# Four transposed pieces or one: turning back the weighted values in layers three and four of an eight-block transformer kernel

## The reference, cut to what matters

```python
# 16 heads of 8 channels, for each head and query
p = exp(q @ k.T * scale - row_max)          # masked: a window of 64, or causal
o = (p @ v) / p.sum(-1)                     # weighted values over the sum of weights
x = x + o.reshape(T, 128) @ W_o             # projection and residual
```

## Time and profile before

| | us |
|---|---|
| runs | 1268.28, 1269.37, 1276.36 |
| median | 1269.37 |
| profiled execution, first to last instruction (span) | 1288.7 |
| of it, layers three and four up to the routing's end, about | 520 to 1190 |

### The profile page before, as it was taken

The page is one execution under the profiler, slowest core; times in us unless marked ns, Lnnn a source line. Parts: engine busy times, 40 slices in busy tenths (PEclk is TensorE's granted clock), DMA queues, the critical chain, the costliest instruction groups (busy, mean ns, idle before and its releaser), DMA issues.

```text
span 1288.7 us, 39126 instructions
## 1 busy us (share of the span) xinstructions
PE 1079.1 (84%) x16755; PEld 784.4 (61%) x16755; DVE 832.1 (65%) x2425; ACT 551.8 (43%) x993; POOL 448.7 (35%) x538
## 2 busy tenths in 40 slices
PE   6989868999976996887888888888888888897994
PEld 4767647888864673644555656565555655453884
DVE  6888674678974213367768786877858685635332
ACT  3332102366552331324473836556374645361442
POOL 3134341436655253122221333142223203012575
PEclk9898869999986998898999999998999999898998
DMA  9554505652240413103021222211122201101884
GB/s 369 203 214 176 202 27 180 199 177 87 71 162 31 136 54 94 47 26 89 18 76 37 53 81 54 61 47 55 45 61 61 64 6 27 42 13 61 214 199 91
DMA packets 85167, 126.05 MB, mean 98 GB/s; under 512 B 14465, under 2 KB 66050, under 8 KB 84578
## 3 DMA queue, kind: packets, MB, share of 16 engines
q1 hardware_dynamic: 68258, 106.47, 25.8%
q0 software_dynamic: 10928, 13.64, 4.4%
q10 hardware_dynamic: 5808, 3.43, 1.1%
HBM read 50.82 MB, written 46.74 MB: 76 GB/s over the span
## 4 chain that ended last, share of the span: by engine, by line
PE 44%; DVE 22%; issue 9%; ACT 7%; DMA 6%; SPq 4%; POOL 4%; another core or an unknown queue 1%; ACTq 0%; DVEq 0%; POOLq 0%
DVE mx L1714 5%; SPq L2238 3%; PE ps L1058 3%; PE ps L1025 3%; ACT MW L1998 3%; PE ps L790 2%; PE ps L777 2%; PE ps L778 2%; PE ps L613 2%; PE ps L739 2%; DMA K<-spm 2%; ACT MW L1985 2%; DVE bst L1137 2%; PE ps L965 1%; DVE MW L1516 1%
## 5 line engine op out<-in xcount | busy, mean ns | idle before, releaser
L1714 DVE TENSOR_REDUCE mx<-ps 128x2 f32<-128x1024 f32 (+3 forms) x176 | 191.8, 1122 | 64.2 <-PE ps L1025 60.0
L1998 ACT ACTIVATE MW<-ps 128x1024 f32<-128x1024 f32 x160 | 154.6, 1036 | 87.8 <-PE ps L1042 87.3
L2136 POOL DMA_INDIRECT xs<-xr,sidu x96 | 97.1, 1011 | 134.2 <-DVE sidu L1296 99.1
L2079 POOL TENSOR_SCALAR rst<-bmv 128x4 f32<-128x4 f32 x64 | 16.3, 255 | 267.4 <-DVE bmv L1140 266.4
L1025 PE MATMUL ps<-K,Q 64*128 64x512 bf16 (+3 forms) x512 | 66.9, 324 | 27.7 <-DMA K<-spm 16.8
L1058 PE MATMUL ps<-MW,Vp 128*18 128x128 f32 x2560 | 88.5, 281 | 1.7 <-ACT MW L1998 1.2
L1058 PEld LDWEIGHTS ps<-MW,Vp 128*18 128x18 f32 x2560 | 65.0, 100 | 12.8 <-issue 4.7
L2162 POOL DMA_INDIRECT out_dram<-qf,toku x39 | 60.6, 1555 | 34.5 <-DVE toku L1770 25.9
L1985 ACT ACTIVATE MW<-ps 128x1024 f32<-128x1024 f32 x64 | 61.8, 1028 | 17.5 <-PE ps L951 15.3
L1042 PE MATMUL ps<-Q,K 64*128 64x128 bf16 x1280 | 55.9, 220 | 14.7 <-ACT MW L1998 7.1
L1803 ACT COPY XT<-ps 128x512 f32<-128x512 f32 x48 | 28.3, 590 | 87.9 <-PE ps L613 78.3
(11 more groups left out here) (381 smaller groups left out, 2606.5 us busy)
## 6 DMA issues: line engine op xcount, KB each, us to landing
xs<-hb SPq DMA_DIRECT2D x52, 528.0 KB, 8.6
MW<-l_moe_dram SPq DMA_DIRECT2D x19, 768.0 KB
MW<-l_moe_dram SPq DMA_DIRECT2D x20, 578.0 KB
Q<-spl SPq DMA_DIRECT2D x48, 128.0 KB
Q<-spm SPq DMA_DIRECT2D x48, 128.0 KB
K<-spl SPq DMA_DIRECT2D x43, 128.0 KB
K<-spm SPq DMA_DIRECT2D x43, 128.0 KB
MW<-l_moe_dram SPq DMA_DIRECT2D x16, 256.0 KB
```

The costliest lines, as they stand in the source:

```text
L1714: V.tensor_reduce(out=mx[1][:, :, s0:s0 + ns, t], in_=p.rearrange("p (e n) -> p e n", e=2)[:, :, 0:ns * nk].rearrange("p e (s k) -> p e s ...
L1998: A.activation(P3[k % 2][:, 1024 * half:1024 * half + 1024], p, ACT.Exp).then_inc(drained[u], 1)
L2136: G.indirect_dma_start(out=xs[L], out_offset=bass.IndirectOffsetOnAxis(ap=sidu[:, 4 * b + t:4 * b + t + 1], axis=0), in_=src[:, t, :], in_ ...
```

## The change

The four pieces become one step, `l2_t` or `l3_t`. It waits for the four tiles in turn, turns all eight halves into one unit (the full two banks), and DVE then takes one reciprocal of 64 numbers per partition and one product of 512. There are 16 such steps instead of 64. The step stands in the lists of PE and DVE where the last of its four pieces stood; with the pieces left out, all five engines' lists are the same step for step. `l3_t` of the last block keeps the two throw-away matmuls, now ahead of all eight transposes.

```diff
@@ ORDER2, one line of PE's list of many
-        l3_lat l3_q l3_e2 l3_b1 l3_k l3_e3 l3_b2 l3_v l3_t0 l2_m3 l3_e4 l3_b3 l3_t1 l3_e5 l3_b4 l2_n2 l3_e6 l3_b5 l3_e7 l2a_n l3_b6 l3_m0 l3_e8
...
-            ("l3_n2", B - 1): 4, ("l3_t3", B - 1): 2, ("l3f_n", B - 1): 3}
+            ("l3_n2", B - 1): 4, ("l3_t", B - 1): 2, ("l3f_n", B - 1): 3}
...
-    UNITS |= {f"{_t}_t{_i}": 1 for _i in range(4)} | {_t + "_u": 1, _t + "_j": 1}
+    UNITS |= {_t + "_t": 1, _t + "_u": 1, _t + "_j": 1}
@@ PE
-            def out_t(key, l, t):
+            def out_t(key, l):
                 u, n, p = unit(key)
-                rows = opb[l][t]
                 ahead(key)
-                e.wait_ge(og_out[l], 4 * key[1] + t + 1)
-                for g in range(2):
-                    m = PE.transpose(p[:, 128 * g:128 * g + 128], rows[:, g, :], ident)
+                for t in range(4):
+                    e.wait_ge(og_out[l], 4 * key[1] + t + 1)
+                    for g in range(2):
+                        m = PE.transpose(p[:, 256 * t + 128 * g:256 * t + 128 * g + 128], opb[l][t][:, g, :], ident)
                 m.then_inc(filled[u], 1)
@@ DVE
-            def out_t(key, l, t):
+            def out_t(key, l):
                 u, n, p = unit(key)
-                k = 4 * l + t
-                pv = p[:, 0:256].rearrange("p (q r) -> p q r", q=8)[:, :, 0:18].rearrange("p q (k e) -> p q k e", k=2)
-                rd = rdens[k].rearrange("p (q k) -> p q k", q=8)
-                if t == 0 and key[1]:
+                pv = p.rearrange("p (q r) -> p q r", q=32)[:, :, 0:18].rearrange("p q (k e) -> p q k e", k=2)
+                rd = rden[:, 64 * l:64 * l + 64].rearrange("p (q k) -> p q k", q=32)
+                if key[1]:
                     ukey = (key[0][:2] + "_u", key[1] - 1)
                     e.wait_ge(filled_of(ukey), after(ukey))
                 e.wait_ge(filled[u], n + 1)
                 own.end(V.reciprocal(rd, pv[:, :, :, 8]))
                 settled()
-                V.tensor_tensor(out=tcs[l][:, t, :].rearrange("p (q k e) -> p q k e", q=8, k=2), in0=pv[:, :, :, 0:8], in1=bc(rd, 3, [128, 8, 2, 8]),
+                V.tensor_tensor(out=tcs[l].rearrange("p t (q k e) -> p (t q) k e", q=8, k=2), in0=pv[:, :, :, 0:8], in1=bc(rd, 3, [128, 32, 2, 8]),
                                 op=ALU.mult).then_inc(drained[u], 1)
```

More of the change, by code:

```diff
@@ L219 @@
-        l3_m21 l3_n2 l3_e0 l3_e1 l3_b0 l3f_n l3_e2 l3_b1 l3t_r l3_e3 l3_t0 l3_b2 l3_e4 l3_b3 l3_e5 l3_b4 l3_e6 l3_b5 l3_t1 l3_e7 l3_b6 l3_e8 l3t_c
-        l3_b7 l3_e9 l3_b8 l3_t2 l3_b9 l3_t3 l3_u l3_j l3f_n l3t_r l3t_c
+        l2a_n l2_q l2a_n l2_v l2_m0 l2_m1 l2_m2 l2_m3 l2_n2 l2_q l2_e0 l2_e1 l2_o0 l2_e2 l2_o1 l2_e3 l2_o2 l2_o3 l2_t l2_u l2_j l2_v l2f_n l2f_0
+        l2f_1 l2f_2 l2_m0 l2f_o l2_m1 l2_m2 l3a_n l3_q l3_lat l2a_n l3_k l2_m3 l2_q l3_v l2_n2 l3_m0 l3_m1 l3_m2 l3_m3 l3_m4 l2_e0 l3_m5 l2_e1 l3_m6
@@ new lines @@
+        l3_m7 l2_o0 l3_m8 l2_e2 l3_m9 l3_m10 l2_o1 l3_m11 l3_m12 l2_o2 l3_m13 l2_e3 l3_m14 l3_m15 l2_o3 l2_t l3_m16 l2_u l3_m17 l2_j l3_m18 l2_v
+        l3_m19 l2f_n l3_m20 l3_m21 l2f_0 l2f_1 l2f_2 l3_n2 l2_m0 l2f_o l3_e0 l2_m1 l3_e1 l3_b0 l3a_n l2_m2 l3_lat l3_q l3_e2 l3_b1 l3_k l3_e3 l3_b2
+        l3_v l2_m3 l3_e4 l3_b3 l3_e5 l3_b4 l2_n2 l3_e6 l3_b5 l3_e7 l2a_n l3_b6 l3_m0 l3_e8 l3_b7 l3_m1 l3_e9 l3_b8 l3_m2 l3_m3 l2_q l3_m4 l3_b9 l3_m5
+        l2_e0 l3_m6 l2_e1 l3_m7 l3_m8 l2_o0 l3_m9 l2_e2 l3_m10 l2_o1 l3_m11 l2_e3 l3_m12 l3_m13 l2_o2 l3_t l3_m14 l2_o3 l3_m15 l3_u l2_t l3_m16
@@ new lines @@
+        l2f_o l3_e0 l2_m1 l3_e1 l3_b0 l3f_n l3a_n l2_m2 l3_q l3_lat l3_e2 l3_k l3_b1 l3_b2 l3t_r l3_e3 l2_m3 l3_e4 l3_b3 l3_e5 l3_b4 l3t_c l3_e6 l3_v
+        l3_b5 l2_n2 l3_e7 l3_m0 l3_m1 l3_b6 l2a_n l3_m2 l3_e8 l3_b7 l3_m3 l3_e9 l3_b8 l3_m4 l3_m5 l2_q l3_m6 l2_e0 l2_e1 l3_m7 l2_o0 l3_m8 l3_m9
+        l2_e2 l3_m10 l3_m11 l2_o1 l3_m12 l2_e3 l3_m13 l2_o2 l3_m14 l3_m15 l2_o3 l3_b9 l2_t l3_t l3_m16 l2_u l3_m17 l2_j l3_u l3_m18 l3_j l2_v l3_m19
+        l2f_n l3_m20 l3_m21 l2f_0 l2f_1 l2f_2 l3_n2 l2_m0 l2f_o l3_e0 l2_m1 l3_e1 l3_b0 l3a_n l2_m2 l3_q l3_lat l3f_n l3_e2 l3_k l3_b1 l3_e3 l3_b2
@@ new lines @@
+        l2_m3 l3_e4 l3_b3 l3t_r l3_e5 l3_v l3_b4 l3t_c l3_e6 l3_b5 l2_n2 l3_e7 l2a_n l3_m0 l3_b6 l3_e8 l3_m1 l3_b7 l3_e9 l3_m2 l3_b8 l3_m3 l3_m4 l2_q
+        l3_m5 l3_m6 l3_b9 l3_m7 l2_e0 l2_e1 l3_m8 l2_o0 l3_m9 l2_e2 l3_m10 l2_o1 l3_m11 l2_e3 l3_m12 l3_m13 l3_t l3_m14 l2_o2 l3_m15 l2_o3 l2_t
+        l3_m16 l2_u l3_m17 l2_j l3_u l3_m18 l3_j l2_v l3_m19 l2f_n l3_m20 l3_m21 l2f_0 l2f_1 l2f_2 l3_n2 l2_m0 l2f_o l3_e0 l2_m1 l3_e1 l3_b0 l3a_n
+        l2_m2 l3_q l3_lat l3f_n l3_b1 l3_e2 l3_k l3_e3 l2_m3 l3_b2 l3_e4 l3t_r l3_b3 l3_e5 l3_b4 l3_v l3t_c l3_e6 l2_n2 l3_b5 l3_e7 l2a_n l3_m0 l3_b6
@@ L512, in build @@
         yg1 = hb2[:, 0, :].rearrange("p (t d) -> p t d", t=4)
-        rdens = [rden[:, 16 * k:16 * k + 16] for k in range(8)]
         mw1 = MW[:, 0:4096].rearrange("p (e f) -> p e f", e=8)
@@ L651, in out_u @@
                 u, n, p = unit(key)
-                for t in range(4):
-                    tkey = (f"{key[0][:2]}_t{t}", key[1])
-                    e.wait_ge(drained_of(tkey), after(tkey))
+                tkey = (key[0][:2] + "_t", key[1])
+                e.wait_ge(drained_of(tkey), after(tkey))
                 e.wait_ge(drained[u], n)
```

92 lines of the change are left out of this document (38 added, 54 removed).

## The result

| | kernel before, median (lowest to highest), us | changed kernel | ratio (95%) |
|---|---|---|---|
| first comparison | 1272.68 (1266.48 to 1283.24) | 1282.04 (1271.56 to 1288.74) | 1.0064 [1.0045, 1.0082] |
| second comparison | 1272.21 (1259.90 to 1283.01) | 1277.90 (1273.31 to 1285.53) | 1.0055 [1.0027, 1.0084] |

The changed kernel is slower, by 0.64% or 8.1 us (5.7 to 10.4). That is under the 1% which the prediction took as the least that can be told, but the interval excludes no change, and the second comparison agrees in sign. The forecast was +3.2 us within 1263 to 1279 us, and 1282.04 lies outside. The kernel before came out 3.3 us higher than in the runs shown with the profile; by the ratio alone the forecast's own range, +7.9 at its upper end, just misses the 8.1, and the wider 1263 to 1279 us, +9.6 at its upper end, holds it.

A forecast was written before the change was run, and what follows sets the result against it. Neither PE nor DVE was taken as sole limit; they hand over PSUM units, and DVE often waits for transposes. Terms +1.4 + 0.9 + 3.5 - 2.6 = +3.2 us on 1269.37 gave about 1272 us, eight-in-ten range 1263 to 1279.

The forecast's parts named there:

- the forecast's own range: Whole kernel: -1.8 to +7.9 us, from the ends of the two open terms; 1267 to 1278 us.
- DVE's saving: Sixteen joined steps on DVE: 12.3 us less of its time, about 15 us less in busy sums.
- rival 3: Joined steps' PSUM reciprocal takes 996 ns, DVE saves only 5.2 us, late divisions cost +4: 1276 us; chance 0.10.
- Rival 1: DVE's time bounds the whole stage, so its saving comes through: -11, 1258 us; chance 0.07, half-way case 0.14.
- a shorter 805 to 840: Stretch of layer four's maxima beside window attention: shorter by over a microsecond per block would show Rival 1.
- the three late terms: Division now after the last tile: last block's end +1.4, layer three of block 0 +0.9, blocks 1 to 7 +3.5 us.
- The end of the last block: Strictly serial chain after the throw-away matmuls: six more transposes +0.76 and longer division +0.68, together +1.4 us.
- Layer three of block 0: Serial place: last pair turned 0.24 us later, division 0.68 us longer, together +0.9 us.
- the full stretch: Layer three of blocks 1 to 7, PE and DVE near full: +0.5 us each, +3.5 in all.
- the walk of block 4: Around `l2_o3`: DVE idles from 824.8 to 825.65 awaiting eight transposes, so `m16` begins +0.8 us later.
- the credit of -2.6 us: Exponentials' stretch, seven blocks: half of two departing transpose pairs, 0.37 us a block, leaves the chain.
- rival 2: Row of eight transposes delays the maxima, at `m16` behind `l2_t` or scores behind `l3_t`: +17, 1286 us; chance 0.09.

The follow-up runs named there:

- second comparison: The changed kernel built and timed once more, instruction for instruction, against the kernel before: 1277.90 us, ratio 1.0055 [1.0027, 1.0084].
- second profile before: Profile of the kernel before run once more, instruction for instruction, against itself: 1273.64 us, ratio 1.0017 [0.9985, 1.0050].
- the pairs: Kernel before with layer four's four pieces joined as tiles 0 and 1, and 2 and 3; layer three unchanged: 1275.80 us, ratio 0.9994.
- The halves: Changed kernel with a second PE semaphore after four of eight transposes, DVE dividing in two parts; against the kernel before: 1278.82 us, ratio 1.0051.

## Why the prediction missed, step by step

**Right: the durations and DVE's saving.** 556 + 691 ns for a joined step, 14.0 us less in busy sums where about 15 were said. The row of eight took 0.89 and 1.04 us on the chain, where 1.15 was taken. That the reciprocal does not follow the product's slope held too, and with it rival 3, the reciprocal at 996 ns, is out.

**Right: the time does not follow DVE's total.** Rival 1 is out. Its test was a shorter 805 to 840; the late stretch m13 to m16 became longer instead, 46.4 us against 43.0 and 41.6. That added DVE time does come out in the time, as the doubled reciprocals show, the prediction did not weigh.

**About right in size, in part by luck: the three late terms, forecast +5.8 together.** The end of the last block was put at +1.4; the step itself measured 2.20 - 0.84 = +1.36, and from the last copy of maxima to the last projection's sum the two profiles before have 31.33 and 31.18 us, the changed kernel 32.50 and 33.41, +1.2 to +2.2. Layer three of block 0 was put at +0.9. Before, from the start of ACT's last copy at 540.05, which is also where PE's last product was done, to the end of the division it took 541.31 + 0.30 - 540.05 = 1.56 us:

```profile
541.31 0.30 DVE tco L1683
```

With the change, from the end of PE's last product at 524.47, it is 526.12 + 0.70 - 524.47 = 2.35 us, +0.8:

```profile
521.07 0.89 issue
521.95 0.89 PE ps L958 x46
...
524.47 1.04 PE ps L641 x8
525.51 0.02 issue
525.53 0.57 DVE rden L1673
526.10 0.02 issue
526.12 0.70 DVE tco L1675
```

The 0.89 us at 521.07 is a stall in which PE waited for nothing that the chain shows, in this profile only. From layer three's first maximum to the sum behind this projection the profiles before have 30.09 and 29.93 us, the changed kernel 32.15 and 31.08; without the stall that is +1.0 to +1.3. In the full stretch +3.5 was forecast. From m13 to m16 the changed kernel lost 4.8 us over seven blocks against the undisturbed second profile before. From m7 to m13, which `l3_t2` had left, it gained 2.0 to 2.8. Net it lost 2.0 to 2.8 from m7 to m16. The mechanism was as told: DVE idles before the joined step, where it used to have pieces to do. Luck is in the size, since the term was worked out for layer three's steps. With layer three alone joined the place of the walk is 0.8 us longer from m13 to m16, as walked (7.01 against 6.23), but other blocks are shorter by up to 0.95, and the sum is 42.0 against 41.6. Layer four alone brings it to 47.8.

In the walk of block 4 one step was off, though. It had the row of transposes begin 0.3 us before DVE's maxima end (824.5 and 824.8), since both pairs ahead of `l2_o3` were to bring it forward by 0.36 us each. It begins 0.29 us after them (811.08 and 810.79), so DVE idles 1.42 us and not 0.85. The pair right ahead of `l2_o3` had held PE at no cost: `l2_o3` needs ACT's copy of the tile before, and that one ended at 823.21, with the pair's hold ending at 823.34.

```profile
822.97 0.44 PE L647 MATMUL ps<-W,tmpA 128*128 128x128 f32 x2
823.34 1.09 PE L965 MATMUL ps<-MW,Vp 128*18 128x64 f32 x64
```

```profile
822.82 0.39 ACT L2005 COPY tmpA<-ps 128x256 f32<-128x256 f32 x1
```

With the pair gone PE idles there, 0.58 us `<-ACT tmpA L1997` in the lines above, and starts at 809.19 behind this copy:

```profile
808.76 0.38 ACT L1997 COPY tmpA<-ps 128x256 f32<-128x256 f32 x1
```

**Failed: the credit of -2.6 us in "What goes from the chain".** It said that `l3_t0` and `l3_t1` leave the stretch of exponentials with nothing in their place and that half of what they held on the chain comes back. The chain did show them there. But no gain shows where they left: that stretch took 241.3 and 235.7 us in the changed kernel, 234.5 and 238.2 before, 238.9 with the pairs that leave them there. Over all kernels without doubled work the mean is 236.9 us where they left (nine profiles) and 237.0 where they stayed (five). A difference of 2.6 is two standard errors of such means, so the sum over all blocks does not quite exclude it. Five of the seven passages, those from blocks 0 to 4, scatter less, and there the means are 168.8 and 169.0: 0.2 us where five sevenths of the credit would be 1.9, with a standard error of 0.7. What the runs show in place of the credit is no gain at the place left, and a loss for the move as a whole: moving layer four's pieces with nothing joined costs 0.72% [0.32, 1.12]. A row on the chain tells that an instruction was on it in that execution; it does not tell that the next limit is as much earlier. What the next limit was in that stretch no run here shows; around `l2_o3` it was ACT's copy, as above.

**Failed with it: how the move was entered.** The sum took the gain at the place which the pieces left and priced the place which they enter only through layer three's steps; layer four's row of eight, in a stretch where PE had 89% and DVE 85%, stood in rival 2 alone, with 0.09. Yet joining layer three alone costs nothing that can be told, and layer four alone all of it. Rival 2's place was right (the division between `m13` and `m16`, and the wait for the row), its size was not: it had +17, the runs have +8.1. Its test, over 10 us more idle time in front of L1714, did not trigger: the page gives

```profile
DVE mx L1706 <- PE ps L1018: 62.0, 57, 7.7
```

after 60.0 us before, or 54.4 in the second profile. The loss lies in longer work between the maxima and in idle time in front of the reciprocal at a few places, which that total hides, since over the run its wait fell to 27.0 us.

The Trainium skill ("Perfetto Trace Analysis", section on optimizing Scalar/DVE operations) says that grouping can help throughput where the engine is saturated, and that smaller instructions may finish sooner where it is not but holds others up. The sign agrees with the second half. The reason does not quite: the moved but unjoined pieces are as small as before and cost at least as much. The halves did let DVE start 0.44 us sooner at one place, and took 0.50 more. What counted was where the instructions stand more than their size.

**How the 8.1 us stand to what is located.** Ends +1.0 to +1.3 and +1.2 to +2.2, m7 to m16 +2.0 to +2.8: 4.2 to 6.3 us. The remaining 2 to 4 us lie within the scatter of single profiles, in the stretch of exponentials above all (5.6 us between two profiles of the changed kernel), and stay open. From the last projection's sum to the end both profiles of the changed kernel have 123.8 us and those before 121.9 and 122.6, but other kernels lie anywhere from 122.0 to 123.9. The split stays open too, between the stretch that `l3_t0` and `l3_t1` left and the place that they entered: tiles 0 to 2 joined also take them out of the stretch of exponentials and gave 1.0027 [0.9995, 1.0060], which neither proves a cost nor excludes one. And it stays open why layer four alone measured 1.0090 and the whole change 1.0064; their intervals overlap.

## What to carry to other kernels

A joined step stands where the last of its parts stood, so before its saving is counted, write down which stretch the early parts leave and which they enter, and price both; time leaving a stretch is a gain only if nothing else holds that stretch. Test the order by itself, with the parts moved and not joined: this one edit settled here what a count of saved instructions could not. When an experiment changes the time, look at the granted clock of its runs before pricing an engine by it. The price of adding an engine's time, measured by doubling an instruction, is no price for taking time away by a change that also reorders.

## What the runs showed of the hardware

- A reciprocal of 64 numbers per partition read from PSUM with gaps (columns 8 and 17 of every 32) takes 556 ns, as much as one from SBUF (553 ns). With 16, 32, 48 and 64 numbers it takes about 250, 347, 460 and 556 ns. Of the shapes between, all with two signals, and the first with three tiles joined:

```profile
L1714 DVE RECIPROCAL rden<-ps x32: 345/347/359, 526.1 to 1154.0; 128x32 f32<-128x32 f32 x32
```

```profile
811.61 0.46 DVE L1712 RECIPROCAL rden<-ps 128x48 f32<-128x48 f32 x1
```

- Doubling the reciprocal in the changed kernel put 9.4 us on DVE and about 18 us on the time. In its profiled execution the granted clock over 508 to 1175 us was 0.93, where the two profiles of the changed kernel have 0.95 and 0.97:

```profile
508.00:1175.00 667.00, 550.40 (x11221) 375.13 (x11220) 439.84 (x904) 333.30 (x534) 167.88 (x222) 0.93 0.18 47
```

  Its six runs have 0.934 on average, the changed kernel's beside it 0.944. By the slope of 8 us for 0.01 that makes up an estimated 8 us, the rest of the 18. Why the clock is lower no run here shows.
- Profiles of one and the same kernel differ by up to 13.6 us in span (1288.7 and 1275.1), more than this change is worth. The granted clock and where a few stalls of 1 to 4 us fall vary from one execution to the next.
